# A click-model tower on one core: whole-array transposes of the pair products, the last product on quarters, products between the last fills, and a tenth one-hot table in four blocks

## What is computed

```python
e = stack([tbl_f[ids[:, f]] for f in range(26)], axis=1)      # 2048 x 26 x 128
c = concatenate([e, r_dense_x[:, None, :]], axis=1)           # 2048 x 27 x 128
z = einsum('bfd,bgd->bfg', c, c)[:, triu_i, triu_j]           # 2048 x 351
h = concatenate([z, r_dense_x], axis=1)                       # 2048 x 479
h = maximum(h @ W_top1 + b_top1, 0)                           # 512 wide
h = maximum(h @ W_top2 + b_top2, 0)                           # 256 wide
y = h @ W_top3                                                # 1 wide
```

## Time and profile before

| | us |
|---|---|
| runs, median of 3 | 390.56 (390.32 to 392.99) |
| profiled execution | 390.03 |
| its span, first to last instruction | 388.2 |
| TensorE products busy / weight loads busy | 354.7 / 321.3 |
| VectorE busy | 222.7 |
| ScalarE busy | 174.0 |
| GpSimd busy (272 gathers) | 264.9 |
| granted clock, mean | 0.996 |

### The profile page before, as it was taken

The page is one execution under the profiler, slowest core; times in us unless marked ns, Lnnn a source line. Parts: engine busy times, 40 slices in busy tenths (PEclk is TensorE's granted clock), DMA queues, the critical chain, the costliest instruction groups (busy, mean ns, idle before and its releaser), DMA issues.

```text
span 388.2 us, 14394 instructions
## 1 busy us (share of the span) xinstructions
PE 354.7 (91%) x6432; PEld 321.3 (83%) x6432; DVE 222.7 (57%) x253; ACT 174.0 (45%) x483; POOL 264.9 (68%) x280
## 2 busy tenths in 40 slices
PE   2887979998999999999999999998999989989787
PEld 2776868987889888988889888888989888978676
DVE  4786898944568535763568535763568534821122
ACT  2437236545436173544436273444446253453422
POOL 6777787767777777777777777777777777773000
PEclk9999999999999999999999999999999999998999
DMA  6777415323232323232222322223231322221000
GB/s 177 234 221 210 120 46 136 71 78 82 63 84 56 82 65 85 56 82 52 80 68 58 83 63 84 57 76 85 69 84 50 83 65 55 58 57 37 2 3 0
DMA packets 17566, 31.25 MB, mean 80 GB/s; under 512 B 5720, under 2 KB 8672, under 8 KB 17504
## 3 DMA queue, kind: packets, MB, share of 16 engines
q0 software_dynamic: 8704, 17.84, 18.4%
q1 hardware_dynamic: 7920, 11.68, 10.0%
q10 hardware_dynamic: 880, 0.80, 0.7%
HBM read 30.29 MB, written 0.01 MB: 78 GB/s over the span
## 4 chain that ended last, share of the span: by engine, by line
PE 78%; DMA 8%; DVE 5%; ACT 5%; issue 3%; SPq 0%; ACTq 0%; DVEq 0%
PE x_ps L618 34%; PE tail_ps L702 16%; PE gram_ps L637 13%; DMA hot_in<-in_tbl 8%; PE x_ps L599 6%; DVE onehot L894 3%; PE tail_ps L662 3%; PE tail_ps L674 2%; ACT xt L394 2%; PE tail_ps L708 2%; DVE hot_lo L880 1%; ACT xt L841 1%; ACT gram L416 1%; PE x_ps L742 1%; PE tail_ps L753 0%
## 5 line engine op out<-in xcount | busy, mean ns | idle before, releaser
L582 POOL DMA_INDIRECT raw<-in_tbl,ids_sb x272 | 264.1, 971 | 88.8 <-issue 82.4
L894 DVE TENSOR_TENSOR onehot<-ids_wide,row_ps 128x1024 fp32r<-128x1024 int16 (+1 forms) x160 | 180.5, 1163 | 61.9 <-PE x_ps L618 58.1
L618 PE MATMUL x_ps<-onehot,hot_hi 128*128 128x256 f32 x566 | 147.1, 295 | 4.0 <-DVE onehot L894 1.3
L618 PE MATMUL x_ps<-onehot,hot_lo 128*128 128x256 f32 x566 | 139.7, 282 | 0.4 <-issue 0.4
L618 PEld LDWEIGHTS x_ps<-onehot,hot_hi 128*128 128x128 f32 x566 | 106.6, 188 | 11.7 <-ACT xt L394 3.9
L618 PEld LDWEIGHTS x_ps<-onehot,hot_lo 128*128 128x128 f32 x566 | 106.7, 188 | 0.5 <-issue 0.5
L394 ACT COPY xt<-x_ps 128x128 f32<-128x128 f32 (+1 forms) x99 | 47.8, 565 | 47.8 <-PE x_ps L618 47.2
L637 PE MATMUL gram_ps<-xt 128*27 128x26 f32 x4096 | 52.4, 192 | 9.6 <-issue 5.7
L637 PEld LDWEIGHTS gram_ps<-xt 128*27 128x27 f32 x4096 | 43.6, 104 | 18.7 <-issue 11.4
L599 PE MATMUL x_ps<-ident,raw 128*128 128x128 f32 x272 | 40.9, 279 | 7.8 <-ACT xt L394 7.2
L416 ACT COPY gram<-gram_ps 128x416 f32<-128x416 f32 (+1 forms) x32 | 16.2, 506 | 66.8 <-PE gram_ps L637 66.8
(11 more groups left out here) (90 smaller groups left out, 339.6 us busy)
## 6 DMA issues: line engine op xcount, KB each, us to landing
raw<-in_tbl,ids_sb POOLq DMA_INDIRECT x272, 2.6
ids_wide<-in_hot_ids SPq DMA_DIRECT2D x17, 256.0 KB
hot_in<-in_tbl SPq DMA_DIRECT2D x14, 256.0 KB, 3.5
weights_in_place<-in_w SPq DMA_DIRECT2D x12, 128.0 KB, 2.4
hot_in<-in_tbl SPq DMA_DIRECT2D x4, 320.0 KB, 4.0
dense_sb<-in_dense_t ACTq DMA_DIRECT2D x6, 128.0 KB, 2.6
dense_sb<-in_dense_t SPq DMA_DIRECT2D x2, 128.0 KB, 4.1
ids_wide<-in_hot_ids SPq DMA_DIRECT2D x1, 192.0 KB
```

The lines of the kernel that those rows point to most:

```text
L582: nc.gpsimd.indirect_dma_start(out=raw[k][:, f, :], out_offset=None, in_=sources[f], in_offset=bass.IndirectOffsetOnAxis(ap=ids_sb[:, t, f ...
L618: last = nc.tensor.matmul(ps, table[:, chunk_at[j] + c, :], moving[:, c - a, :], start=(c == 0 and table is tables_of[0]), stop=(c == chun ...
L894: nc.vector.tensor_tensor(columns(p), ids_wide[:, it // IDS % IDS_RING, it % IDS, 0:width].unsqueeze(1).to_broadcast([P, n, width]), row_n ...
```

## The change

- `HOT` is 10, and `SHARES` is (1, 1, 0, 1, 0, 1, 0, 0): the tenth table (1250 rows, 10 chunks) is gathered in blocks 0, 1, 3 and 5, and taken by one-hot products in blocks 2, 4, 6 and 7. There are 264 gathers. A tile of these four blocks has 16 gathered tables in four groups of four. The table is loaded last, and its residue is made when it is first used (`late`).
- "zt" has two steps. The first transposes 128 columns of both halves of `z` at once with the whole array, into one bank (`z[:, s, 0:128]`); the second transposes the remaining 64 columns of the upper half and multiplies the remaining 41 of the lower half with the identity, into the other. `z` is 192 columns wide, ten of them set to zero in the opening (`z_padded`). ScalarE and VectorE read both sets of the first step in one instruction. The rows of the first weights are arranged for it.
- "y" is made of four quarters of 64 samples, each on its own column strip, and lies on partitions 0, 32, 64 and 96. It is copied with 97 partitions by 64, and stored as four rows.
- The step "y" stands behind the last row transposes of its stretch, not before them.
- In the last block, two empty places stand between the two fills of tile 14, which the tail of block 6 may use. Starts 0 and 1 of the last h1 stand between the two fills of tile 15, and the dense residue of the last block with them.

```diff
-HOT = 9
+HOT = 10
-SHARES = (0,) * 8
+SHARES = (1, 1, 0, 1, 0, 1, 0, 0)
...
-    return first, [j for j in first if j not in direct] + direct, direct
+    late = [j for j in first if j < SHARES[0]]
+    return first, [j for j in first if j not in direct + late] + direct + late, direct
...
-    rest = 64
-    z_blocks = [[(0, slice(0, half_pairs[0] - rest))], [(1, slice(0, P))],
-                [(1, slice(P - rest, half_pairs[1])), (0, slice(half_pairs[0] - rest, half_pairs[0]))]]
-    n_kz = len(z_blocks)
-    kz = [blk[0][1].stop - blk[0][1].start for blk in z_blocks]
+    z_wide = P + P // 2
+    n_zt = 2
+    kz = [P, P, half_pairs[1] - P // 2]
+    n_kz = len(kz)
+    zt_of = [0, 0, 1]
...
-            slots += gram_slots(t) + with_turn([[] for _ in range(n)], t + 1, list(range(n)))
+            fills_of = gram_slots(t)
+            slots += fills_of[:1] + [[], []] + fills_of[1:] + with_turn([[] for _ in range(n)], t + 1, list(range(n)))
...
-        slots += gram_slots(t + 1, hot[lead:lead + beside])
+        slots += gram_slots(t + 1, hot[lead:lead + beside] if hot else [[("start", 0), ("start", 1)], []])
...
-            before.setdefault(tail_from[h] + min(int(at * n / span[-1]), n - 1), []).append(("tail", h, key, part))
+            place = n if key[0] == "y" else min(int(at * n / span[-1]), n - 1)
+            before.setdefault(tail_from[h] + place, []).append(("tail", h, key, part))
...
+        def zt_parts(j, ps, of):
+            if j == 0:
+                return (ps.rearrange("p (s o g) -> p o g s", s=QUAD, o=2),
+                        of[:, 0:2, :].rearrange("p o (g s) -> p o g s", s=QUAD))
+            return (ps[0:kz[2], 0:BLOCK].rearrange("p (s g) -> p g s", s=QUAD),
+                    of[0:kz[2], 2, :].rearrange("p (g s) -> p g s", s=QUAD))
+
+        def y_copy(act, h, ps):
+            reach(act, y_stored, 16 * h)
+            nc.scalar.copy(y_sb[0:3 * y_rows + 1, :], ps[0:3 * y_rows + 1, 0:y_cols]).then_inc(y_copied, 1)
+            act.wait_ge(y_copied, h + 1)
+
+        def y_store(act, h):
+            act.dma_start(out[:, h * BLOCK:(h + 1) * BLOCK].rearrange("o (s n) -> (o s) n", n=y_cols),
+                          y_sb[0:3 * y_rows + 1:y_rows, :]).then_inc(y_stored, 16)
...
+            def y_products(ps, c):
+                for s in range(4):
+                    last = nc.tensor.matmul(ps[s * y_rows:s * y_rows + 1, 0:y_cols], w3_sb[:, c:c + 1],
+                                            h2[:, c, s * y_cols:(s + 1) * y_cols], start=(c == 0), stop=(c == m2 - 1))
+                return last
...
+                            pe.wait_ge(z_padded, 1)
...
-                    if part > 0:
-                        pe.wait_ge(rest_turned, h + 1)
+                    upper, lower = slice(0, groups_block), slice(groups_block, P)
                     for s in range(QUAD):
-                        for bank_of, (odd, of) in zip((ps, tail_ps[tail_bank["zt", 1]]), blocks_of):
-                            rows = slice(odd * groups_block, (odd + 1) * groups_block)
-                            last = nc.tensor.transpose(
-                                bank_of[0:of.stop - of.start, s * groups_block:(s + 1) * groups_block],
-                                z[rows, s, of], ident[rows, rows])
+                        if j == 0:
+                            last = nc.tensor.transpose(ps[:, s * P:(s + 1) * P], z[:, s, 0:P], ident[:, :])
+                        else:
+                            of_s = slice(s * groups_block, (s + 1) * groups_block)
+                            nc.tensor.transpose(ps[0:P // 2, of_s], z[upper, s, P:z_wide], ident[upper, upper])
+                            last = nc.tensor.matmul(ps[P // 2:kz[2], of_s], z[lower, s, P:half_pairs[1]],
+                                                    ident[lower, lower], start=True, stop=True)
...
-            last_start(0)
             tail_step(h, ("cols", 0), 0)
             tail_step(h, ("cols", 1), 0)
-            last_start(1)
             tail_step(h, ("cols", 2), 0)
             tail_step(h, ("cols", 3), 0)
             last_start(2)
             tail_step(h, ("zt", 0), 0)
             tail_step(h, ("zt", 1), 0)
             last_start(3)
-            tail_step(h, ("zt", 2), 0)
-            for m in range(m1):
-                last_h1_with_hi(m, 0)
-            tail_step(h, ("zt", 2), 1)
+            for k in range(n_kz - 1):
+                for m in range(m1):
+                    last_h1_with_hi(m, k)
...
-                last = nc.tensor.matmul(last_y, w3_sb[:, m:m + 1], h2[:, m, :], start=(m == 0), stop=(m == m2 - 1))
+                last = y_products(last_y, m)
...
+            nc.vector.memset(z[0:groups_block, :, half_pairs[0]:z_wide], 0.0).then_inc(z_padded, 1)
...
+                elif kind == "start" and what == [0]:
+                    dense_residue(dve, blocks - 1)
```

More of the change, by code:

```diff
@@ L707, in tail_step, with last_start @@
                         pe.wait_ge(tail_copied[h2_bank], h * tail_per[h2_bank] + tail_nth["h2", c] + 1)
-                        last = nc.tensor.matmul(ps[0:1, 0:BLOCK], w3_sb[:, c:c + 1], h2[:, c, :],
-                                                start=(c == 0), stop=(c == m2 - 1))
+                        last = y_products(ps, c)
                 if part == parts[key] - 1:
                     last.then_inc(tail_full[kind], 1)
+            h = blocks - 1
+            of = [slice(m * P, (m + 1) * P) for m in range(m1)]
+            def last_start(m):
+                nc.tensor.matmul(last_h1[m], ident[:, :], b1_sb[:, m:m + 1].to_broadcast([P, BLOCK]), start=True, stop=False)
+                for weights, part in ((w1z_hi, dense_hi), (w1z_lo, dense_hi), (w1z_hi, dense_lo)):
+                    if m == 0:
+                        pe.wait_ge(dense_rounded if part is dense_hi else dense_split, h + 1)
+                    nc.tensor.matmul(last_h1[m], weights[:, n_kz, of[m]], part[h % DENSE][:, :], start=False, stop=False)
             pe.wait_ge(ident_ready, 1)
@@ L725, in _ @@
                     tail_step(*what)
+                elif kind == "start":
+                    last_start(*what)
                 elif kind == "gram":
                     products(*what)
-            h = blocks - 1
-            of = [slice(m * P, (m + 1) * P) for m in range(m1)]
-            def last_start(m):
-                nc.tensor.matmul(last_h1[m], ident[:, :], b1_sb[:, m:m + 1].to_broadcast([P, BLOCK]), start=True, stop=False)
-                for weights, part in ((w1z_hi, dense_hi), (w1z_lo, dense_hi), (w1z_hi, dense_lo)):
-                    if m == 0:
-                        pe.wait_ge(dense_rounded if part is dense_hi else dense_split, h + 1)
-                    nc.tensor.matmul(last_h1[m], weights[:, n_kz, of[m]], part[h % DENSE][:, :], start=False, stop=False)
             def last_h1_with_hi(m, k):
-                pe.wait_ge(zt_rounded, h * n_kz + k + 1)
+                pe.wait_ge(zt_rounded, h * n_zt + zt_of[k] + 1)
                 for weights in (w1z_hi, w1z_lo):
@@ L855, in _ @@
             h = blocks - 1
-            for key in tail[:n_cols + n_kz]:
+            for key in tail[:n_cols + n_zt]:
                 if key[0] != "cols" or tail_bank[key] == 0:
@@ L865, in _ @@
             act.wait_ge(last_y_full, 1)
-            act.wait_ge(y_stored, 16 * h)
-            copy(y_sb[:, :], last_y).then_inc(y_copied, 1)
-            act.wait_ge(y_copied, blocks)
-            act.dma_start(out[:, h * BLOCK:(h + 1) * BLOCK], y_sb[:, :]).then_inc(y_stored, 16)
+            y_copy(act, h, last_y)
+            y_store(act, h)
         @block.vector
```

68 lines of the change are left out of this document (27 added, 41 removed).

## The result

| | us |
|---|---|
| before, median of 20 runs beside it | 392.19 (390.32 to 395.45) |
| after, median of 20 runs | 394.72 (393.09 to 398.89) |
| ratio, with 95% interval | 1.0106 (1.0080 to 1.0132) |
| profiled execution of after | 398.89, span 396.9 |

386.0 was forecast, with a range up to 391; by the ratio the change costs 4.1 us (1.06% of 390.56). The ratio compares fast runs alone; the medians, which take in all runs, lie 2.5 us apart.

The account below looks back on a forecast made before the run. TensorE's own instruction stream was taken as the bound from about 99 us, with gathers ahead. Terms +8.6 + 0.5 - 6.5 - 0.6 - 4.0 - 2.0 = -4.0 us took the profiled 390.03 to 386.0; own range 383 to 388.7, with rivals 380 to 391.

Parts of the forecast that it names:

- What bounds the kernel: From about 99 us TensorE's own instruction stream sets the pace; gathers run ahead, by 9.9 us at tile 14.
- Part 1: Tenth one-hot table in blocks 2, 4, 6, 7: +2.15 us a block, +8.6 in four, and +0.5 in the opening.
- the rival on the slower side: The table brings a 2.54 us kind of wait into each of its four blocks: +10.2, 396.2 us; chance 0.10.
- Part 2: Last product (y) on quarters, side by side on four column strips: 0.35 instead of 0.96 us, -0.6 a tail.
- Part 3: Pair transposes (zt) in each tail: 1.1 to 1.2 us instead of 1.8, no wait for the first bank, -0.7 a tail.
- Parts 4 and 5: From the last tile pair to the last block -4.0 us; from there to the last store -2.0 us.
- the lower clock behind the first: Behind the 1.63 us wait at tile 14, clock 0.50 from 352.0 to 354.4 loses 1.2 us; to vanish.
- part 5: The end, 365.61 to the last store: starts moved between the last fills -1.4, y -0.6; sum -2.0 us.
- it hung on the count of instructions: Tile 14's wait of 1.63 stays, and with it the lower clock: +2.8, 388.8 us; chance 0.17.
- Sum: Whole change: +8.6 + 0.5 - 6.5 - 0.6 - 4.0 - 2.0 = -4.0 us, giving 386.0.

Follow-up runs that it names:

- x1: The changed kernel without the tenth table (nine tables, 272 gathers), all else as changed; ratio to before 0.996 (0.9926 to 0.9994).
- x6: The kernel before with y on quarters at its old place, nothing else; ratio to before 1.0103 (1.0032 to 1.0175).
- x13: The kernel before with y, still four long instructions, moved behind the last row transposes; ratio to before 0.9883 (0.9805 to 0.9962).
- x2: The changed kernel with the four half transposes grouped ahead of the four plain products; ratio to before 1.0007 (0.9970 to 1.0044).
- x11: The kernel before with the new pair transposes alone, half transposes grouped ahead of plain products; ratio to before 0.9968 (0.9939 to 0.9998).
- x9: The kernel before, unchanged, run once more for a second profile; 387.56 us (one run).
- x8: The kernel before with the moved steps at the end alone (tiles 14 and 15); ratio to before 1.0016 (0.9969 to 1.0063).
- x3: The kernel before with the tenth table in blocks 2, 4, 6 and 7 alone; ratio to before 1.0152 (1.0107 to 1.0197).

## Why the prediction was wrong

- **What bounds the kernel** was right: the lead of the gathers grew, and TensorE's waits behind the opening name none of them.
- **Part 1** (+9.1): the term of 2.15 a block is 2.0 in the stretches; the whole is 5.7 to 6.0 us. What is missing lies in part at the end, where the table's slots also take the wait of 1.63 away. The opening, +0.5 in the sum, ended 4.4 us later in the profile of after (103.55 for 99.18), of which the lower clock is some 2.7; x1, without the table and without such a stretch, ends it at 101.15, so the table's share is open. An added wait of 2.54 in each of its blocks, the rival on the slower side, did not come, and yet slower came true.
- **Part 2** (-0.6 a tail): the mechanism was right and its size too (0.74 off y itself). What failed is the step from y's own instructions to the path: in time it gave nothing, with some 0.3 us a tail lost to the fill behind it (x6) and 0.5 us once to the store, "nothing" in the sum. The fill right behind y at the new place is longer with the long y too (x13). The place, costed at nothing, gained about 4.6 us by its ratio and 2.5 by its medians; its own profile does not show where.
- **Part 3** (-0.7 a tail) is the largest miss, some 7 us (-4.3 in the sum with tail 6 and the end, +2.6 measured): it has the wrong sign. Each price was taken from another order than the one it was used for. The 0.09 a piece is busy time over 16 transposes (1.45 / 16), whose real cost from start to start ranges from 0.05 to 0.13 by its group; the 1.8 a tail of before is 1.57; and the new loop, half transposes and plain products in turn, takes 1.63 us (268.12 to 269.75) where the sum had 0.6 to 0.7. So the step went up by 0.6 a tail instead of down by 0.7. The prediction weighed changeovers for y alone, where they did not matter, and not for the transposes, where they did. That the order is the cost is shown by grouping (x2, 0.91 us for the same instructions); that the gain grouped is small, by x11.
- **Parts 4 and 5**: the waits did vanish with the new order. But they hang on places in the code, and the lower clock behind the first (1.2 us of the sum) need not follow: x9 has the wait, 1.05 instead of 1.63, without it. The end alone measured +0.6 us (-1.2 to +2.5) where the sum had about -3.8 for it (-1.63, -1.2, and -1.0 of part 5). The rival "it hung on the count of instructions" was half right: the count sets the place; what sets the length is open. The end itself did get shorter (40.8 us in x8, 43.5 and 42.1 in before); why the time did not is open, since the wait in x8's tile 10 is in x13 too.
- **Sum**, measured: table +5.7, quarters 0, place -4.6, transposes +2.6, end +0.6: +4.3; after is +4.1. That these agree to 0.2 is luck: the place is known to 3 us either way, the end to 2, and the quarters, 0 here, cost up to 1% with the old transposes. The table's cost and that of the order are shown; the rest of the sum is not settled.

## What to carry to other kernels

Cost an instruction in the order it will stand in, from start to start: the same twelve instructions took 1.63 us in turn and 0.91 in groups here, so group by kind before judging the idea. A wait with no releaser in a dense run of small instructions stood at a place that moved with the code, and came and went there: shift the code and run the kernel again before crediting a change with its disappearance. Time each part of a bundle alone, and then some of them together; here two losses (1.5% and 1.0%) hid a gain of 1.5%, and the parts of that gain do not add up in every order.

## What the hardware showed unexpectedly

- Two small products between half transposes take 0.23 us until the next transpose starts; in series eight of them take 0.57 (268.17 to 268.74 in x2), 0.14 for two. A half transpose takes 0.17 between such products and 0.085 in series (267.83 to 268.17). Yet half transposes that take the two halves of the array in turn, into two banks, take 0.05 each (257.31 to 257.70 in before).
- A fill can take 1.20 us (360.84 to 362.04 in after, behind pair transposes; about as much behind h1 products, and behind a wait of 0.91 in x3), 9.4 ns a product; in the middle of a dense stream the same 128 products take 1.7, and right behind y at the new place 2.2 to 2.4 in the mean. That this is the supply of instructions is argued, not shown.
